# Cross attentions 0 and 1 of a four-layer Perceiver kernel: value products in two blocks a step, and two small copies on ACT

## The reference, cut to what matters

```
x = x + _L0_xattn_ref(_layernorm(x), ctx, mask, q_w, q_b, k_w, k_b, v_w, v_b)   # layer 0
x = x + _L1_xattn_ref(_layernorm(x), ctx, mask, Wq, Wk, Wv, Wo)                 # layer 1
# in both:
q, k, v = heads(x @ q_w), heads(ctx @ k_w), heads(ctx @ v_w)    # 16 heads of 16
scores  = einsum('bhqd,bhkd->bhqk', q, k) / 4                    # masked keys left out
probs   = softmax(scores)
out     = einsum('bhqk,bhkd->bhqd', probs, v)
```

## Time and profile before

| | |
|---|---|
| median of 3 runs | 2418.33 us (2417.73 to 2421.09) |
| the profiled execution | 2417.08 us, its span 2415.8 us |
| TensorE (PE) busy | 2043.5 us, 85% of the span |
| VectorE (DVE) busy | 1480.4 us, 61% |
| ScalarE (ACT) busy | 1167.1 us, 48% |
| 31 of the 32 steps of attention 0 | 469.91 us, from 94.93 us on |
| 31 of the 32 steps of attention 1 | 466.57 us, from 860.11 us on |
| mean granted TensorE clock | 0.931 of full speed; 0.99 and 1.00 in the two attentions |

### The profile page before, as it was taken

The page is one execution under the profiler, slowest core; times in us unless marked ns, Lnnn a source line. Parts: engine busy times, 40 slices in busy tenths (PEclk is TensorE's granted clock), DMA queues, the critical chain, the costliest instruction groups (busy, mean ns, idle before and its releaser), DMA issues.

```text
span 2415.8 us, 36542 instructions
## 1 busy us (share of the span) xinstructions
PE 2043.5 (85%) x13415; PEld 1181.7 (49%) x13415; DVE 1480.4 (61%) x3559; ACT 1167.1 (48%) x2491; POOL 625.2 (26%) x822
## 2 busy tenths in 40 slices
PE   5999999997965799999999889997976887947766
PEld 2544554443543444554444455466455775624443
DVE  2576567785775267666777474422377996674362
ACT  2466656665333256556666441332335883614131
POOL 4232223300570523222320230000232442513040
PEclk8999999998986899999999889998998999978988
DMA  6455445551010645544642203431012321101100
GB/s 167 88 134 114 108 94 126 109 137 36 1 39 31 104 108 127 118 93 106 151 83 38 72 4 117 140 100 45 1 64 76 97 79 37 47 13 40 43 1 13
DMA packets 122547, 187.25 MB, mean 78 GB/s; under 512 B 22632, under 2 KB 70305, under 8 KB 122017
## 3 DMA queue, kind: packets, MB, share of 16 engines
q1 hardware_dynamic: 122368, 184.92, 30.8%
HBM read 131.86 MB, written 2.13 MB: 55 GB/s over the span
## 4 chain that ended last, share of the span: by engine, by line
PE 68%; DVE 21%; ACT 4%; issue 2%; POOL 2%; SPq 1%; DMA 1%; DVEq 0%; ACTq 0%; POOLq 0%
PE PS L701 10%; PE PS L657 9%; PE PS L683 9%; PE PS L307 8%; PE PS L315 6%; PE PS L624 5%; DVE WK L757 4%; PE PS L612 4%; DVE WK L2025 3%; PE PS L1554 2%; PE PS L1579 2%; PE PS L409 2%; PE PS L457 2%; PE PS L436 2%; ACT WK L508 2%
## 5 line engine op out<-in xcount | busy, mean ns | idle before, releaser
L757 DVE TENSOR_REDUCE WK<-PS 128x1 f32<-128x1024 f32 x512 | 618.8, 1221 | 353.7 <-PE PS L657 351.4
L849 ACT ACTIVATE WK<-PS 128x512 f32<-128x512 f32 x1024 | 548.5, 599 | 236.3 <-PE PS L683 228.4
L683 PE MATMUL PS<-WK 100*128 100x256 bf16 x2048 | 342.7, 275 | 1.8 <-ACT WK L849 1.5
L657 PE MATMUL PS<-WK 100*128 100x512 bf16 x1024 | 306.1, 382 | 24.4 <-DVE WK L757 22.7
L683 PEld LDWEIGHTS PS<-WK 100*128 100x128 bf16 x2048 | 171.0, 98 | 237.4 <-issue 111.3
L701 PE MATMUL PS<-WK 128*32 128x256 f32 x3072 | 206.2, 385 | 0.0
L508 ACT ACTIVATE WK<-PS,WK 128x256 f32<-128x256 f32 (+1 forms) x320 | 140.6, 451 | 75.5 <-DVE WK L476 45.2
L885 POOL TENSOR_SCALAR WK<-WK 128x2 bf16<-128x2 f32 x64 | 14.1, 220 | 596.8 <-PE PS L683 519.4
L534 POOL TENSOR_TENSOR WK<-WK 128x128 f32<-128x128 f32 (+1 forms) x128 | 65.0, 508 | 370.8 <-DVE WK L494 308.4
L701 PEld LDWEIGHTS PS<-WK 128*32 128x32 f32 x3072 | 80.5, 109 | 102.4 <-issue 50.5
L657 PEld LDWEIGHTS PS<-WK 100*128 100x128 bf16 x1024 | 91.2, 98 | 69.3 <-DVE WK L757 55.0
(11 more groups left out here) (317 smaller groups left out, 3407.9 us busy)
## 6 DMA issues: line engine op xcount, KB each, us to landing
WK<-WK SPq DMA_DIRECT2D x768, 64.0 KB
WB<-in_ctxT SPq DMA_DIRECT2D x78, 512.0 KB, 4.8
WK<-in_ctxT SPq DMA_DIRECT2D x40, 512.0 KB, 3.7
WA<-in_ctxT SPq DMA_DIRECT2D x26, 512.0 KB, 4.7
WK<-in_ctx SPq DMA_DIRECT2D x8, 1024.0 KB, 5.7
WK<-in_ctx SPq DMA_DIRECT2D x16, 512.0 KB, 3.9
WK<-scratch_q SPq DMA_DIRECT2D x12, 256.0 KB, 8.3
WB<-in_L3f_qkv SPq DMA_DIRECT2D x2, 1536.0 KB, 6.7
```

Source lines behind the costliest of these rows:

```text
L657: x = pe.e.matmul(b.ap[:, u, :], QS[0:100, h, bb * 256 + q * 128:bb * 256 + (q + 1) * 128], KS[s % 4][0:100, c * 1024 + u * 512:c * 1024 + ...
L683: x = pe.e.matmul(b.ap[:, j * 256:j * 256 + 256], KS[s % 4][0:100, kt * 128:(kt + 1) * 128], QS[0:100, h, bb * 256:bb * 256 + 256], start= ...
L757: dv.e.tensor_reduce(mt[:, n:n + 1], tile["R", L, s, n].rearrange("p a b -> p (a b)"), AX, ALU.max).then_inc(*dv.at("R", L, s, n))
L849: ac.e.activation(PR[n % NPR], tile["S", L, s, i], ACT.Exp).then_inc(*ac.at("E", L, s, i))
```

## The change

The generator gives two F blocks a step in place of four, each of 16 key tiles: F(s,0) behind S(s,10), F(s,1) behind S(s+1,2). M(s+1) moves from behind S(s,13) to right behind F(s,0), K from behind S(s,9) to behind S(s,6), V from behind S(s,5) to behind S(s,14). R runs one tile further ahead: during step s R(s+1, 5..7) and R(s+2, 0..4) are issued, and the head of the program issues 13 instead of 12. ACT instead of DVE makes M's copy of three rows and the copy E0 of the products.

```diff
-    for n, r in enumerate(first[:12]):
+    for n, r in enumerate(first[:13]):
...
             yield "S", s, i
             if i % 2 == 0:
-                n = 4 + i // 2 if i < 8 else i // 2 - 4
-                if s + (1 if i < 8 else 2) < 32:
-                    yield "R", s + (1 if i < 8 else 2), n
-            if i == 1 and s:
-                yield "F", s - 1, 3
-            if i == 2 and s and s + 1 < 24:
-                yield "L", s + 1
+                ahead, n = (1, 5 + i // 2) if i < 6 else (2, i // 2 - 3)
+                if s + ahead < 32:
+                    yield "R", s + ahead, n
             if i == 2 and s:
+                if s + 1 < 24:
+                    yield "L", s + 1
+                yield "F", s - 1, 1
                 yield "E0", s - 1
-            if i == 5 and 8 <= s < 16:
+            if i == 6 and s < 24:
+                yield "K", s // 4 + 2, s % 4
+            if i == 10:
+                yield "F", s, 0
+                yield "M", s + 1
+            if i == 14 and 8 <= s < 16:
                 yield "V", 1, s - 8, s
-            if i in (6, 10, 14):
-                yield "F", s, i // 4 - 1
-            if i == 9 and s < 24:
-                yield "K", s // 4 + 2, s % 4
-            if i == 13:
-                yield "M", s + 1
...
-                    for kt in range(8 * c, 8 * c + 8):
+                    for kt in range(16 * c, 16 * c + 16):
...
-                        dv.wait_ge(pe, "M", L, s, 1)
-                        dv.e.tensor_copy(QS[96:99, h, bb * 256:bb * 256 + 256],
-                                         tile["M", L, s][:, 0, :].bitcast(BF)[96:99, 0:256]).then_inc(*dv.at("M", L, s))
...
-                    dv.e.tensor_copy(PVS, bank[7].ap[:, 0:256]).then_inc(*dv.at("E0", L, s))
...
+                    ac.wait_ge(pe, "M", L, s, 1)
+                    ac.e.activation(QS[96:99, h, bb * 256:bb * 256 + 256],
+                                    tile["M", L, s][:, 0, :].bitcast(BF)[96:99, 0:256], ACT.Copy).then_inc(*ac.at("M", L, s))
...
+                    ac.e.activation(PVS, bank[7].ap[:, 0:256], ACT.Copy).then_inc(*ac.at("E0", L, s))
```

More of the change, by code:

```diff
@@ L141, in xattn_order @@
             if i % 2 == 0:
-                n = 4 + i // 2 if i < 8 else i // 2 - 4
-                if s + (1 if i < 8 else 2) < 32:
-                    yield "R", s + (1 if i < 8 else 2), n
-            if i == 1 and s:
-                yield "F", s - 1, 3
-            if i == 2 and s and s + 1 < 24:
-                yield "L", s + 1
+                ahead, n = (1, 5 + i // 2) if i < 6 else (2, i // 2 - 3)
+                if s + ahead < 32:
+                    yield "R", s + ahead, n
             if i == 2 and s:
+                if s + 1 < 24:
+                    yield "L", s + 1
+                yield "F", s - 1, 1
                 yield "E0", s - 1
-            if i == 5 and 8 <= s < 16:
-                yield "V", 1, s - 8, s
-            if i in (6, 10, 14):
-                yield "F", s, i // 4 - 1
-            if i == 9 and s < 24:
-                yield "K", s // 4 + 2, s % 4
-            if i == 13:
-                yield "M", s + 1
+            if i == 6 and s < 24:
[4 more added lines that the diff above has]
+            if i == 14 and 8 <= s < 16:
+                yield "V", 1, s - 8, s
         if s + 4 < 32:
             yield "ST", s + 4
-    yield "F", 31, 3
+    yield "F", 31, 1
     yield "E0", 31
@@ L661, in xattn_pe @@
                     s = o[1]
-                    b = take2(rr, ("M", L, s), (dv, "ME", L, s))
+                    b = take2(rr, ("M", L, s), (dv, "ME", L, s), *([(ac, "M", L, s)] if s < 32 else []))
                     settle(b)
@@ L670, in xattn_pe @@
                     if s >= 2:
-                        pe.wait_ge(dv, "E0", L, s - 2)
+                        pe.wait_ge(ac, "E0", L, s - 2)
                         for q in range(2):
@@ L679, in xattn_pe @@
                     settle(b)
-                    pe.wait_ge(dv, "M", L, s)
+                    pe.wait_ge(ac, "M", L, s)
                     for j in range(2):
@@ L690, in xattn_pe @@
                         if s:
-                            pe.wait_ge(dv, "E0", L, s - 1)
+                            pe.wait_ge(ac, "E0", L, s - 1)
                         else:
@@ L694, in xattn_pe @@
                                 pe.wait_ge(*event)
-                        pv.owner = ((dv, "E0", L, 31),)
+                        pv.owner = ((ac, "E0", L, 31),)
                         pe.wait_ge(ac, "V", L, bb, 7)
-                    for kt in range(8 * c, 8 * c + 8):
+                    for kt in range(16 * c, 16 * c + 16):
                         n = 16 * s + kt // 2
@@ L766, in xattn_dve @@
                     s = o[1]
-                    if s < 32:
-                        g, hh, bb, h = where(s)
-                        dv.wait_ge(pe, "M", L, s, 1)
-                        dv.e.tensor_copy(QS[96:99, h, bb * 256:bb * 256 + 256],
-                                         tile["M", L, s][:, 0, :].bitcast(BF)[96:99, 0:256]).then_inc(*dv.at("M", L, s))
                     if s >= 2:
@@ L849, in xattn_act @@
                     ac.e.activation(PR[n % NPR], tile["S", L, s, i], ACT.Exp).then_inc(*ac.at("E", L, s, i))
+                elif o[0] == "M" and o[1] < 32:
+                    s = o[1]
+                    g, hh, bb, h = where(s)
+                    ac.wait_ge(pe, "M", L, s, 1)
+                    ac.e.activation(QS[96:99, h, bb * 256:bb * 256 + 256],
+                                    tile["M", L, s][:, 0, :].bitcast(BF)[96:99, 0:256], ACT.Copy).then_inc(*ac.at("M", L, s))
+                elif o[0] == "E0":
+                    s = o[1]
+                    ac.wait_ge(pe, "F", L, s, 7)
+                    if s:
+                        ac.wait_ge(pe, "E1", L, s - 1, 1)
+                    ac.e.activation(PVS, bank[7].ap[:, 0:256], ACT.Copy).then_inc(*ac.at("E0", L, s))
         def xattn_pool(L):
```

## The result

The changed kernel takes 2472.91 us in the median of 4 runs (2469.35 to 2474.30), the kernel before 2418.03 beside it: ratio 1.022, 95% interval 1.0205 to 1.024, or 55 us slower. Forecast were 43 us more. The profiled execution's span is 2472.9 us for 2415.8 before.

The account below looks back on a forecast made before the run. TensorE, 97 to 98% busy, was taken to wait for two R slots and three score banks. Attention 0's 17.9, attention 1's 13.1 and loads' 12 gave +43 us on 2417.1: 2461, range 2440 to 2482.

Parts of the forecast that it names:

- The block's borders: Each value block F loses 0.24 us at its two borders; two fewer blocks save 0.48 us a step.
- Rival A: The block saving comes through without new waits: 31 us faster, 2387 us; chance 0.12.
- New R waits: Row-maximum tiles R wait for VectorE's slots ahead of the long F, so a plain step gains only 0.18 us.
- the walk: The prediction's start-by-start timing of TensorE through each kind of step after the change; plain step 12.44 us for 12.62.
- The bank wait behind K: In key steps S10 waits 0.64 us for a score bank; steps grow 0.35 (attention 1) or 0.55 (attention 0).
- Key and value steps: Behind V, S2 waits 0.75 us for a bank; with the key half, +1.07 (attention 1) or +1.27 (attention 0).
- Copies on ACT: The two small copies moved from VectorE to ACT are covered by ACT's idle time; price nil.
- Rival B: Small ACT copies delay exponentials, 0.3 us each, twice a step: 38 us more, 2499 us; chance 0.04.
- The landing keys: K's second copy waits for DMAs reading its buffer, in five steps per attention: about 12 us, ends 4 and 21.
- The last two steps: The two short last steps of each attention: exponentials set them already, so the change costs nil.
- regular steps: Key, key and value, and plain steps together: +17.9 us in attention 0 and +13.1 in attention 1.
- Rival C: About even: the new waits cost half of those walked, leaving +6 us, 2424 us; chance 0.07.

Follow-up runs that it names:

- E0: Not a run: code name of the copy of the products out of bank 7, which the change moves from DVE to ACT.

## Why the prediction was right, point by point

- **The block's borders.** Predicted 0.24 a block. A long block is followed at 1.86 (1274.79 to 1276.65, above) for the predicted 1.87, so 0.48 a step did go from TensorE's work: its busy time fell by 0.40 in a key step. By the drain of about 0.175 us that the Trainium skill (TensorE: Matmul & The Clock Gate, Single matmul latency) gives, a block would have been worth an estimated 0.35; the rows keep to 0.24. Rival A's saving is real and was not lost on TensorE itself.
- **New R waits.** Plain step forecast -0.18, measured -0.26 (12.36). The R of a plain step stand where the walk put them: 0.87, 1.05 and 1.32 apart from R7 on (forecast 0.87, 1.04, 1.33), and F follows at 3.78 (forecast 3.77). The 0.08 too much is M, which follows the block at 1.77 (1339.53 to 1341.30) where the walk has 1.87. R in threes without a block between them eats about half of the 0.48. Spreading R took 0.29 more off a plain step.

```profile
1335.75 0.59 PE L655 MATMUL PS<-WK 100*128 100x512 bf16 x2
...
1338.99 0.61 PE L655 MATMUL PS<-WK 100*128 100x512 bf16 x2 [0.26 <-DVE WK L755]
1339.53 1.93 PE L699 MATMUL PS<-WK 128*32 128x256 f32 x32
1341.30 0.27 PE L666 MATMUL PS<-idb,WK 128*3 128x128 bf16 x2
```

- **The bank wait behind K.** S10 forecast 1.74 behind S7, measured 1.75 (1211.13 to 1212.88). Key steps forecast 14.94 and 15.14, measured 14.87 and 15.04. Shown by the move of one tile.
- **V.** S2 forecast 1.84 behind S15, measured 1.83 (1132.45 to 1134.28). Key and value steps forecast 19.43 and 19.63, measured 19.33 and 19.52. Shown by V moved alone.
- **Copies on ACT.** Forecast nil; shown in both orders for every kind of step. M's copy takes 0.38 and E0's 0.38, near the row of 0.39. Rival B falls.
- **The landing keys.** Forecast 12 us of waits; the copies waited 6.2 + 7.2 = 13.4. That they pass into the step without slack was right as well. What the step left out is what such a pause does to TensorE: in attention 0 three drops of the clock behind pauses. The ten steps, with the step behind one of them, are 13.6 and 7.9 us over their kinds, 21.5 in all, so attention 1, where the clock held, pays 7.9 for 7.2 us of waiting, and attention 0 pays 13.6 for 6.2. This term was sized 12 and measures about 20, with the 1.4 taken off that steps 16, 17 and 20 of attention 0 already lost before. The run with K behind S9 in these ten steps gives the same: there they keep 1.4 us over their kinds, so again 20 had gone with the waits. This is the largest mis-sized term of the sum, and in attention 1 later landings have a part in it.
- **The last two steps.** Forecast nil. The last but one is 11.50 for 10.83, and the last lasts 1.6 longer, from its first S to the last transposes (564.84 to 576.32 before, 595.10 to 608.18 after): 4.5 us for both attentions. They have no R, exponentials set their pace, and ACT starves while TensorE is in a long block: in the last step it idled 0.34 behind a block before, and 1.46 behind the long one. With the copies back on VectorE the step is as long (13.04 for 13.08), so it is not the copies. No run tested the block alone in these steps. This is the step of the sum that was wrong in kind, not only in size.

```profile
569.70 2.07 ACT L849 ACTIVATE WK<-PS 128x512 f32<-128x512 f32 x4 [0.34 <-PE PS L683]
```

```profile
604.19 2.56 ACT L836 ACTIVATE WK<-PS 128x512 f32<-128x512 f32 x5 [1.46 <-PE PS L681]
```

The sum of regular steps measures 15.1 + 10.7 us for the forecast 17.9 + 13.1; landing keys add 20 and the ends 4.5. The two profiled executions differ by 57.1 us (spans 2472.9 and 2415.8), and the attentions with their ends hold 49.4 of them. The other 7.7 lie outside: 3.4 ahead of the first step (98.31 for 94.93, of which TensorE's first matmul, at 13.3 us for 12.2, has 1.1), 2.2 between the attentions and 2.2 behind the second. The last two stretches vary by 3 and 4 us among the kept traces, so they need no cause in the change; none of the three was traced further. That the total came within 12 us of the forecast is in part luck: the regular steps were forecast 5 us too slow, which took off some of the 12 that landing keys and ends were too low.

Rival C, that half of the waits would appear, falls with every kind of step.

## What to carry to other kernels

In an in-order program with n buffers, look at the user n + 1 places behind a piece whose evacuation occupies the consuming engine (here the fourth score tile behind a projection, with three banks): the first user behind the piece is emptied late, and that one needs its buffer. Something long, here the value block, has to lie between the projection and it. Merging work saves its borders only if the work that is fed meanwhile is spread again, since a longer block is also a longer silence for the engines behind. And where a trace already shows waits of 0.4 to 1.3 us at a place, moving the waiting instruction 0.6 us earlier, to where no slack is behind it, puts the whole wait into the step.

## What the runs showed of the hardware that had not been expected

In the changed kernel a pause of TensorE of 2.1 to 2.4 us, in an attention whose key steps are otherwise 92% busy, came with a fall of the granted clock from 1.00 to 0.50 (2.4 to 1.2 GHz) in step 4 of attention 0, for the 3.30 us shown, and again in steps 8 and 20. The pause of 2.17 us in step 16 and pauses of 2.55 and 2.53 us in attention 1 brought none. It is not the attention that decides: with the copies back on VectorE step 20 of attention 1 had a fall, behind a pause of 2.26. In step 8 the idle time of 2.44 us was followed by this:

```profile
233.61 0.60 PE L681 MATMUL PS<-WK 100*128 100x256 bf16 x2 [2.44 <-ACT WK L836]
234.01 1.06 PE L655 MATMUL PS<-WK 100*128 100x512 bf16 x2
235.00 3.64 PE L699 MATMUL PS<-WK,WB 128*32 128x256 f32 x32
```

3.64 us for 1.93. With a wait of 1.66 us on ACT that step came to 4.6 us over its kind. With the copies back on VectorE the wait in the same step was 1.50, the clock stayed at 1.00 and the excess was 1.8 (21.27), so most of the difference is the clock's. Removing the waits (K behind S9 in every fourth step) kept the clock at 1.00, and past the first step of an attention no kept trace has a fall without such a pause; so the fall needs the pause, and the pause alone does not bring it. What else it takes is open.

A key projection can also wait for its own input. With K moved by one tile, and in the kernel of before with the copies on ACT, step 18 of attention 1 waited for context to land, 1.9 and 1.6 us:

```profile
1181.43 1.94 PE L610 MATMUL PS<-WB 128*64 128x512 f32 x8 [1.92 <-DMA WB<-in_ctxT]
```

```profile
1163.53 1.94 PE L612 MATMUL PS<-WB 128*64 128x512 f32 x8 [1.57 <-DMA WB<-in_ctxT]
```

Three other traces have 0.7 to 1.0 us of it in the same step, and the kernel before and the changed kernel have none. The second kernel above has the lengths of before in every kind of step, so a single execution can probably differ by this much without a cause in the change; no run shows what decides it.
